# Causal attention on one core: the narrow diagonal steps' probabilities joined into GpSimd's tile of sums

## The reference, cut to what matters

```python
scores = jnp.einsum('bhsd,bhtd->bhst', qh, kh) * scale
mask = jnp.triu(jnp.ones((Sq, Sq), dtype=bool), k=0).at[0, 0].set(False)
scores = jnp.where(mask, -jnp.inf, scores)
probs = jax.nn.softmax(scores, axis=-1)
out = jnp.einsum('bhst,bhtd->bhsd', probs, vh)
```

## Time and profile before

| | us |
|---|---|
| median of 3 runs | 1460.29 (1458.22 to 1466.49) |
| the profiled execution, device time | 1449.43 |
| its span in the profile | 1447.7 |
| PE busy | 1271.4 (88% of the span) |
| POOL busy | 582.6 (40%) |
| mean granted clock of TensorE | 0.929 |

### The profile page before, as it was taken

One profiled execution on the slowest core, in us unless ns is written; L12 is line 12 of the kernel. 1 busy time (PEld: TensorE's weight loads), 2 busy tenths in 40 slices (PEclk: granted clock), 3 DMA queues, 4 the chain that ended last, 5 costly groups with the idle time before them and its releaser, 6 DMA issues. The chain is left out here.

```text
span 1447.7 us, 29708 instructions
## 1 busy us (share of the span) xinstructions
PE 1271.4 (88%) x11456; PEld 901.2 (62%) x11456; DVE 887.5 (61%) x2318; ACT 619.2 (43%) x1191; POOL 582.6 (40%) x799
## 2 busy tenths in 40 slices
PE   6999999949899999999999999936888778789998
PEld 5888888824455555555555555315666577788887
DVE  6555555236577777777777777224767645566665
ACT  3222222104455555555555555512333235355553
POOL 0000000023576676666666666724555324212220
PEclk9999999958999999999999999968999956668998
DMA  7555665377245555555555550047666455224443
GB/s 259 215 203 203 217 218 203 145 182 169 57 93 112 118 117 117 118 117 118 118 118 117 118 117 17 16 126 267 210 207 212 138 159 195 92 87 123 151 141 117
DMA packets 164607, 210.85 MB, mean 146 GB/s; under 512 B 8960, under 2 KB 96768, under 8 KB 162944
## 3 DMA queue, kind: packets, MB, share of 16 engines
q1 hardware_dynamic: 150656, 190.25, 45.9%
q10 hardware_dynamic: 13824, 18.88, 3.6%
HBM read 131.24 MB, written 77.59 MB: 144 GB/s over the span
## 5 line engine op out<-in xcount | busy, mean ns | idle before, releaser
L716 ACT ACTIVATE p_t<-p_bank 128x512 f32<-128x512 f32 (+1 forms) x608 | 312.2, 586 | 242.4 <-PE p_bank L774 238.2
L755 PE MATMUL p_bank<-k_stack,q_stack 96*128 96x512 f32 (+3 forms) x768 | 284.8, 394 | 31.2 <-DMA ident<-in_ident 19.3
L662 DVE CUSTOM_DVE_ANT_0 tried<-p_bank,ban 128x128 bf16<-128x128 f32 (+3 forms) x512 | 237.6, 486 | 105.8 <-PE p_bank L755 104.4
L774 PE MATMUL p_bank<-q_stack,k_stack 97*128 97x512 f32 (+3 forms) x768 | 261.7, 360 | 18.3 <-DMA q_stack<-m_row 11.9
L755 PEld LDWEIGHTS p_bank<-k_stack,q_stack 96*128 96x128 f32 x768 | 146.4, 194 | 154.4 <-issue 64.0
L665 DVE TENSOR_REDUCE mx_a<-p_bank 128x1 f32<-128x512 f32 x256 | 175.9, 687 | 64.8 <-PE p_bank L755 63.4
L774 PEld LDWEIGHTS p_bank<-q_stack,k_stack 97*128 97x128 f32 x768 | 146.0, 192 | 53.7 <-ACT p_t L716 26.9
L598 POOL TENSOR_SCALAR_AFFINE_SELECT p_t<-p_t 128x128 f32<-128x128 f32 (+2 forms) x288 | 102.6, 359 | 190.8 <-ACT p_t L716 184.8
L792 PE MATMUL p_bank<-p_t,v_tile 128*32 128x512 f32 (+3 forms) x1536 | 163.5, 498 | 6.8 <-ACT d_sb L700 5.6
L609 POOL TENSOR_TENSOR p_sum<-p_sum,p_t 128x512 f32<-128x512 f32 x128 | 159.9, 1285 | 0.5 <-ACT p_t L716 0.5
L582 POOL MEMSET k_stack<- 1x4096 f32 x3 | 10.4, 3507 | 300.2 <-POOLq L128 300.2
(11 more groups left out here) (130 smaller groups left out, 2483.7 us busy)
## 6 DMA issues: line engine op xcount, KB each, us to landing
q_stack<-q_hi SPq DMA_DIRECT2D x64, 256.0 KB, 6.2
k_stack<-k_hi SPq DMA_DIRECT2D x30, 512.0 KB, 9.0
x_in<-in_x SPq DMA_DIRECT2D x8, 1024.0 KB, 9.2
c_in<-in_ctx_t SPq DMA_DIRECT2D x8, 1024.0 KB, 11.1
k_hi<-k_hi_s SPq DMA_DIRECT2D x8, 1024.0 KB, 4.2
k_lo<-k_lo_s SPq DMA_DIRECT2D x8, 1024.0 KB, 6.4
v_rows<-v_out SPq DMA_DIRECT2D x8, 1024.0 KB, 4.3
q_hi<-q_hi_s SPq DMA_DIRECT2D x8, 1024.0 KB, 4.3
```

What stands on the lines that cost most here:

```text
L662: dve.tensor_tensor_reduce(tried[:, TRIED[c]:TRIED[c] + w], got, ban0[:] if i == 0 else ban[:, CH - w:CH], 1.0, -3e38, ALU.add, ALU.max, t ...
L716: act.activation(pt[:, k % SLOTS_P, u * m:(u + 1) * m, 0:w], bank[:, SB + n % SR, 0:m * w].rearrange("p (m w) -> p m w", m=m), ACT.Exp, sc ...
L755: pe.matmul(bank[:, to, 0:w], qs[it % SLOTS][0:R, i * P // CH, h, i * P % CH:i * P % CH + P], ks[it % SLOTS][0:R, h, t0:t0 + w], start=Tru ...
L774: mm = pe.matmul(bank[:, SB + n % SR, h % m * w:(h % m + 1) * w], ks[slot][0:R + 1, h, j * P:(j + 1) * P], qs[slot][0:R + 1, sh, h, CH - w ...
```

## The change

POOL also adds the probabilities of the two narrow diagonal steps of the second half, step 8 (256 wide) and step 10 (128 wide), into `p_sum`, each with one instruction over all four heads. PE's multiplications by ones for steps 8 and 10 fall away: 8 matmuls in a round. Step 11's multiplication now waits, for all heads, until the last of the round's 14 joins. Step 8 is joined after step 9, and step 10 after step 11. The diff, with the parts that only rename left out:

```diff
-    JOINS = len(FULL) - 1
-    FULL_AFTER = {6: 1, 8: 2, 10: 3}
+    NARROW = [k for k, (_, w) in enumerate(SPAN) if k > 3 and w <= CH // 2]
+    JOINS = 3 * HG + len(NARROW)
+    JOIN_AFTER = {6: (7,), 8: (9, 8), 10: (11, 10)}
+    JOINED = {5: HG, 7: HG, 9: 2 * HG, 8: 2 * HG + 1, 11: 3 * HG + 1, 10: 3 * HG + 2}
...
-                def join(it, n):
-                    if n == 1 and it > 0:
+                def join(it, k):
+                    if k == FULL[1] and it > 0:
                         pool.wait_ge(step_done, it * NS)
+                    if k in NARROW:
+                        c0, w = SPAN[k][0] - CH, SPAN[k][1]
+                        pool.wait_ge(joined, it * JOINS + JOINED[k] - 1)
+                        pool.wait_ge(masked, it * MASKS + MASK0[k] + UNITS[k])
+                        pool.tensor_tensor(p_sum[:, :, c0:c0 + w], p_sum[:, :, c0:c0 + w], pt[:, k % SLOTS_P, :, 0:w],
+                                           ALU.add).then_inc(joined, 1)
+                        return
                     for h in range(HG):
...
-                        if k in FULL_AFTER:
-                            join(it, FULL_AFTER[k])
+                        for i in JOIN_AFTER.get(k, ()):
+                            join(it, i)
...
-                                    if old[1] in FULL:
-                                        act.wait_ge(joined, (old[0] * JOINS + max(1, FULL.index(old[1]))) * HG)
+                                    if old[1] in JOINED:
+                                        act.wait_ge(joined, old[0] * JOINS + JOINED[old[1]])
...
-                    if k in FULL[:-1]:
+                    if k in JOINED and k != FULL[-1]:
                         mm.then_inc(step_done, 1)
...
                         if k == FULL[-1]:
-                            pe.wait_ge(joined, (it * JOINS + JOINS - 1) * HG + h + 1)
+                            pe.wait_ge(joined, (it + 1) * JOINS)
...
                         for k in group:
                             values(it, k)
-                            if k not in FULL[:-1]:
+                            if k not in JOINED or k == FULL[-1]:
                                 sums(it, k)
```

More of the change, by code:

```diff
@@ L599, in mask @@
                                                channel_multiplier=-1).then_inc(masked, 1)
-                def join(it, n):
-                    if n == 1 and it > 0:
+                def join(it, k):
+                    if k == FULL[1] and it > 0:
                         pool.wait_ge(step_done, it * NS)
-                    for h in range(HG):
[L605 to L609, removed]
+                    if k in NARROW:
[5 more added lines that the diff above has]
+                        return
+                    for h in range(HG):
+                        pool.wait_ge(exp_done, it * UNIT0[NS] + UNIT0[k] + h + 1)
+                        if k == FULL[2]:
+                            pool.wait_ge(joined, it * JOINS + h + 1)
+                        if k == FULL[3]:
+                            pool.wait_ge(joined, it * JOINS + 2 * HG + 1)
+                        first = pt[:, FULL[0] % SLOTS_P, h] if k == FULL[1] else p_sum[:, h]
+                        pool.tensor_tensor(p_sum[:, h], first, pt[:, k % SLOTS_P, h], ALU.add).then_inc(joined, 1)
                 def divide(it, half):
```

## The result

| | before | with the change |
|---|---|---|
| median, us | 1459.26 (4 runs, 1458.03 to 1466.49) | 1502.97 (4 runs, 1496.19 to 1509.06) |
| profiled execution, us | 1449.43 | 1507.97 |
| its granted clock, mean | 0.929 | 0.894 |

The changed kernel is slower: ratio 1.0295, 95% interval 1.0236 to 1.0354, or +43.7 us by the medians. The forecast was 1505.6, +45.3. The profiled execution is one of the slower ones of its four, so against the profile of before it is longer by 58.5 us.

A forecast was written before the change was run, and what follows sets the result against it. A round was taken as the longer of PE's way and POOL's chain from first join to sums, plus 17.83 us. Waits of 32.7 and clock of 12.6, together 45.3 us, on the median 1460.29 gave 1505.6; range 1485 to 1522.

The forecast's parts named there:

- The mechanism: At a round's end: the round is the longer of PE's way and POOL's chain to the sums, plus 17.83 us.
- PE's relief at zero: Ahead of step 11's sums: eight matmuls fewer, 0.65 us a round, gain nothing because PE waits there for POOL.
- POOL's adds at 3.75 us a round: Joins of steps 8 and 10 on POOL: 2.39 and 1.29 us, taken as 3.75 with their waits.
- the rival of dearer strips: POOL's new adds take 4.8 us instead of 3.75: 1510 without the clock, 1522 with it; chance 0.09.
- the faster rival: New adds fit in POOL's slack, under 2.28 us together, and PE's relief counts: down to 1450; chance 0.03.
- The steady round at 39.13 us: Rounds 3 to 14: 17.83 + 21.25 + 0.05 = 39.13 us against 37.61, +1.52 each, 18.2 us.
- POOL's slack: Between POOL's last join and PE's load for step 11's sums: 1.46 us in round 9, 2.28 on average.
- The clock: After PE's new stops: a fall in two of three of 15 rounds, 1.26 us each, 12.6 us.
- The rounds without slack: Rounds 0, 1 and 15 pay 3.75 us each, round 2 pays 3.2; together 14.5 us.
- the later mask of step 10: Mask 10 on POOL comes 2.4 us later, but before PE wants it at step 10's values; no cost.
- The base: The 45.3 us, worked out on the profiled execution's 1449.4, were added to the median of 1460.29: 1505.6.
- all rounds would have paid: Rival: the clock falls after the stop in all 15 rounds with following work, 18.9 us: 1512; chance 0.12.

The follow-up runs named there:

- experiment 1: The changed kernel, but PE keeps its sums of steps 8 and 10 beside POOL's new adds; 1489.0 us, ratio 1.0261 against the kernel before.
- experiment 4: The changed kernel with step 11's sums behind the next round's later scores and step 10 joined ahead of step 11; 1465.36 us, ratio 1.0112.
- experiment 2: The kernel before, with PE's sums of steps 8 and 10 dropped and not joined by POOL either; 1449.38 us, ratio 0.9974.
- experiment 11: The kernel before, plus narrow joins and later step 11 sums in rounds 3 to 13, row of maxima ahead of loads from round 3; 1440.36 us, ratio 0.9912.
- Experiment 10: The changed kernel with the next round's row of maxima placed ahead of SP's loads from round 3 on; 1512.53 us, ratio 1.0379.

## Why the prediction was right, and where not

**The mechanism: right.** A round closes over POOL's chain as soon as that outlasts PE's way. Every steady round without a fall takes 38.75 to 38.78 us, whether PE has 8 matmuls more (experiment 1) or not. Moving the wait (experiment 4) brings rounds of 36.9 with the same chain.

**PE's relief at zero: right** for this order (experiment 1). As a gift it is worth 0.80 us a round in the trace of experiment 2, and 4 us by its medians, which is not clear of zero; where no wait takes it, 0.43 us a round are left of it (experiment 11).

**POOL's adds at 3.75 us a round: right.** They measure 2.37 and 1.26, and the chain grew by 21.29 - 17.50 = 3.79 with the waits. The estimate from an element's share of a longer add held; four strips run as one instruction with one start. This rules out the rival of dearer strips, and with it the faster rival, which needed less than 2.28 us. By the estimate from the figure of the Trainium skill (GPSIMD Engine Reference, section 3.1) the adds would have taken 3.4 us; they took 3.63.

**The steady round at 39.13 us: 0.37 too much.** I counted the way from the sums to the next join from the *load* at 721.72, which ran ahead of the matmuls it serves. They could start only behind the values that begin at 721.29; in the earlier trace rows they are not shown, and in the trace they start at 722.15, which leaves 739.55 - 722.15 = 17.40 us. The changed kernel has 17.43. So POOL's slack was larger by as much, 1.89 us in round 9 and 2.71 on average where I had 1.46 and 2.28, and a round without a fall grew by 1.15 instead of 1.52: 12.7 us in eleven rounds where I had 16.7.

**The clock: right in kind, too small in size.** I had two of three rounds fall, and 7 of the 11 steady ones fell. But I priced a fall at 1.26 us, from one that lasted 3.4 us; these last 6.8 and cost 2.1. The share of two in three rested on two stops, one with a fall and one without, so that it came out is luck. The stops themselves were shorter than the 2.2 us I had: 0.96 to 1.95 at the sums of rounds 3 to 13, 1.64 on average. The two errors of steady rounds nearly cancel, which is luck too: 27.6 us measured, where waits and falls together gave 16.7 + 11 x 2/3 x 1.26 = 25.9.

**The rounds without slack: nearly right.** Round 15 paid 3.7 for my 3.75. Rounds 0 to 2 paid 13.4, where I had 10.7 of waits and 3 x 2/3 x 1.26 = 2.5 of clock. I had said that the later mask of step 10 costs nothing. In these rounds it stops PE for 1.9 to 3.6 us; this is the same delay at an earlier place. The clock was granted at 0.96 between 326 and 470 us before and at 0.85 between 326 and 480 with the change; its share and that of the waits were not tried apart. Round 14 paid 5.9 for 1.5 and 0.8 of clock. I had counted it as a round of 37.6 like the others, but it took 35.19 us before; with the change the clock fell twice in it.

**The base.** The profile of before is one of the shortest of its kernel and that of after one of the longer ones (1507.97 of 1496.19 to 1509.06). The medians differ by 43.7 us, the profiles by 58.5, of which 50.6 are in the change's reach. The sum of 45.3 was worked out from rows of that short execution and is 5 us short of what the same rounds show, most of it in round 14. Added to the median it lands within 3 us of the median measured. That is nearer than its parts are, and so in part luck. Of the four runs of the changed kernel, the two at a mean clock of 0.904 and 0.906 took 1496 and 1498 us, and those at 0.894 and 0.898 took 1508 and 1509.

By the loop of the Trainium skill whose every pass loses the clock (TensorE: Matmul & The Clock Gate, section "HAM oscillation — how this bites in real kernels") all rounds would have paid, which at 1.26 us each made 1512. In the change itself four of eleven rounds kept their clock. Experiment 10 comes nearest to such a loop, with ten falls in eleven rounds; that its 1512.53 agrees with the figure is chance, since its falls, at rounds of 40.7 to 41.0 us against 38.73, cost 2.2 each.

## What to carry to other kernels

An engine that is busy for 40% of the span can have no slack: add up its unbroken chain between what it waits for and who waits for it, and compare the gap at its end (1.9 us in round 9 here, 2.7 on average) with the work you mean to add (3.8 us). Work that is taken from the busiest engine ahead of a place where it waits was worth nothing here; move the wait behind other work first. And look at every stop of a microsecond or two on PE, also of a small DMA queued behind large ones: moving one row ahead of the loads gained 1.0% (0.6 to 1.3), where the 10.4 us that the change takes from PE are 0.7% at best.

## What the runs showed of the hardware that I had not expected

- **More work did no harm, and the clock was higher with it.** Experiment 1 has 256 matmul records more than the change, and its clock stays at 1.00 from 480 to 930 us, where the change has 0.95 from 480 to 950. Over the whole program its four runs have 0.913 to 0.916, those of the change 0.894 to 0.906; its median is 1489.0 us against 1502.97, on another chip.
- **Falls repeat over many rounds.** In rounds 4 to 10 of the changed kernel and 4 to 13 of experiment 10 the first joins lie 40.67 to 40.97 us apart: behind a fall in one round comes nearly the same stop, and a fall in the next. In the changed kernel it ended with round 11, for no reason that I know.
- **Falls came in two lengths.** In rounds 3 to 13 of all 13 traces the clock was at 0.50 for about 3.4 or about 6.8 us at a time.
- **A fall isn't a matter of one stop's length alone.** Stops of 1.22 to 2.71 us brought falls, and in round 10 of the fourth experiment the clock fell without any stop longer than 0.55. In the first experiment stops of up to 1.66 us brought none, nor did, in the changed kernel, one of 1.71 (round 3) and one of 1.67 (round 13), in the tenth experiment one of 2.65 (round 3), and in the kernel before one of 2.09. What tells them apart stays open.
